# Pairs of steps added by DMA in SBUF, denominators summed once in four steps, and seven score buffers, in a two-layer graph kernel

## What is computed

```python
h = relu(layernorm(x))                                 # x: 4096 x 64
scores = (h @ W @ a1)[:, None] + (ent @ W @ a2)[None, :]
e = where(scores > 0, scores, 0.2 * scores)            # leaky relu
e = where(adj > 0, e, -9e15)
x = x + elu(softmax(e, axis=1) @ ent + h)              # first layer: attention
h = relu(layernorm(x))
x = x + (adj == 1) @ h + h                             # second layer: sum over neighbours
```

## Time and profile before

| | |
|---|---|
| three runs | 381.06, 383.52, 385.39 us (median 383.52) |
| the profiled execution | 383.43 us, of which the span from first to last instruction is 381.6 us |
| TensorE busy | 348.8 us, 91% of the span |
| VectorE busy | 271.9 us, 71% |
| ScalarE busy | 206.8 us, 54% |
| GpSimd busy | 75.7 us, 20% |
| mean granted TensorE clock | 0.982 of full speed |

### The profile page before, as it was taken

One profiled execution on the slowest core, in us unless ns is written; L12 is line 12 of the kernel. 1 busy time (PEld: TensorE's weight loads), 2 busy tenths in 40 slices (PEclk: granted clock), 3 DMA queues, 4 the chain that ended last, 5 costly groups with the idle time before them and its releaser, 6 DMA issues.

```text
span 381.6 us, 5734 instructions
## 1 busy us (share of the span) xinstructions
PE 348.8 (91%) x2377; PEld 127.6 (33%) x2377; DVE 271.9 (71%) x334; ACT 206.8 (54%) x266; POOL 75.7 (20%) x118
## 2 busy tenths in 40 slices
PE   1598897899878999998998999999999999999996
PEld 1355331123311232332322433332333333335564
DVE  2834949998689898779789776797987977522211
ACT  1120745977567779735767857257668656512100
POOL 5471583222122012022020300000008200001200
PEclk9968899999999999999999999999999999999999
DMA  6999999999999995056029000000000000000011
GB/s 181 182 106 108 108 108 107 107 108 109 106 107 108 106 107 54 2 55 57 0 15 96 3 0 2 0 2 1 2 0 2 0 2 0 2 0 2 2 55 57
DMA packets 10409, 20.67 MB, mean 54 GB/s; under 512 B 1232, under 2 KB 1296, under 8 KB 10128
## 3 DMA queue, kind: packets, MB, share of 16 engines
q0 software_dynamic: 9216, 16.78, 44.3%
q1 hardware_dynamic: 1168, 3.52, 2.5%
HBM read 69.58 MB, written 1.05 MB: 185 GB/s over the span
## 4 chain that ended last, share of the span: by engine, by line
PE 51%; DVE 11%; ACT 4%; issue 3%
PE pb L1223 17%; PE pb L1135 10%; PE pb L1244 9%; PE pa L1135 8%; DVE yp L916 5%; ACT yp L684 2%; DVE coded L828 2%; PE pa L1035 1%; PE pa L1109 1%; PE pa L1103 1%; DVE gmax L797 1%; DVE um L804 1%; PE pa L1099 1%; PE pa L1012 1%; ACT vx L576 1%
## 5 line engine op out<-in xcount | busy, mean ns | idle before, releaser
L684 ACT ACTIVATE yp<-yp,tbias,delta 128x1024 f32<-128x1024 f32 (+1 forms) x160 | 163.6, 1066 | 78.0 <-DVE yp L916 77.9
L916 DVE SCALAR_TENSOR_TENSOR yp<-s8b,t8neg,coded 128x1024 f32<-128x1024 f32 (+1 forms) x160 | 165.7, 1081 | 24.4 <-PE pb L1244 23.2
L1223 PE MATMUL pb<-yp,enta 128*64 128x512 f32 x512 | 136.4, 616 | 15.3 <-ACT yp L684 15.2
L1244 PE MATMUL pb<-yp,onesf 128*32 128x512 f32 x512 | 68.2, 605 | 0.0
L1135 PE MATMUL pb<-am,h 128*64 128x512 fp8e4 x480 | 61.7, 379 | 0.0
L451 POOL DMA_DIRECT2D am<-adj_t x64 | 34.7, 551 | 110.5 <-DMA am<-adj_t 63.2
L1223 PEld LDWEIGHTS pb<-yp,enta 128*64 128x64 f32 x512 | 28.6, 136 | 80.4 <-ACT yp L684 49.0
L1135 PEld LDWEIGHTS pb<-am,h 128*64 128x64 bf16 x480 | 29.1, 110 | 45.1 <-issue 33.5
L828 DVE TENSOR_TENSOR coded<-am,vx 128x2048 uint16<-128x2048 uint16 x32 | 38.9, 1217 | 1.1 <-ACT vx L576 1.1
L513 POOL TENSOR_SCALAR rstd<-rstd 128x8 f32<-128x8 f32 x4 | 3.7, 931 | 157.6 <-ACT rstd L617 157.6
L1135 PE MATMUL pa<-am,h 128*64 128x512 fp8e4 x288 | 34.8, 380 | 0.0
(11 more groups left out here) (165 smaller groups left out, 222.1 us busy)
## 6 DMA issues: line engine op xcount, KB each, us to landing
am<-adj_t POOLq DMA_DIRECT2D x64, 256.0 KB, 26.6
enta<-ent SPq DMA_DIRECT2D x1, 1040.0 KB, 5.1
xs<-xt SPq DMA_DIRECT2D x1, 1024.0 KB, 11.6
out<-yp SPq DMA_DIRECT2D x4, 256.0 KB, 2.0
mats<-eye SPq DMA_DIRECT2D x1, 320.0 KB, 7.1
num<-w_t SPq DMA_DIRECT2D x1, 32.0 KB, 2.0
a_sb<-a_cols SPq DMA_DIRECT2D x1, 0.5 KB, 2.0
```

The source lines that it names most:

```text
L684: e = sc.activation(y, y, ACT.Exp, bias=tbias[:, at:at + 1], scale=delta[:, 0:1])
L916: y = v.scalar_tensor_tensor(out=yp[:, n % YS, r * HALF:r * HALF + W], in0=s8b[:, pair(b) % 2, cols(b)], scalar=t8neg[:, at:at + 1], in1=c ...
L1223: t.matmul(acc2(b)[s * D:(s + 1) * D, :], enta[:, at, 0:D], yp[:, n % YS, s * HALF:(s + 1) * HALF], start=(jt == 0), stop=final, tile_posi ...
L1244: mm = t.matmul(dens[at:at + 32, :], onesf[:, 0:32], yp[:, (n - 1 + r) % YS, s * HALF:(s + 1) * HALF], start=(jt == 1), stop=final, tile_p ...
```

## The change

From step 48 on (`ADD_FROM`), in every group of four steps (4g to 4g+3) that isn't the last of its block, GpSimd issues two DMAs (`add_up`): each adds the buffer of an even step to that of the odd step behind it, in SBUF, after TensorE has done the product of the odd step (`y_read`). Seventeen groups are treated so (12 to 14, 16 to 22, 24 to 30). TensorE sums the denominators of such a group from the two sums in one round, which stands in step 4g+6 (`LAG` = 3), and then counts `pv_done` up by 4. The last group of each block (15, 23, 31) is summed in its own step 4g+3, from all four buffers, in two rounds. VectorE waits for the DMA where it writes over an even step's buffer, and for `pv_done` where it writes over an odd one's. There are 7 score buffers; for their room there are 27 slots instead of 28, and `coded` has one half, so that `put_codes` waits for the scores before it.

```diff
-SLOTS = 28
-YS = 5
+SLOTS = 27
+YS = 7
+ADD_FROM = 48
+LAG = 3
...
+    def closes(g):
+        return 4 * g + 4 in start_of
+
+    ADDED = [g for g in range(STEPS_ALL // 4) if 4 * g >= ADD_FROM and not closes(g)]
+
+
+    def sum_of(n):
+        return 2 * ADDED.index(n // 4) + n % 4 // 2
+
+    def added_by(k):
+        return k % 2, 16 * (k // 2 + 1)
...
-        coded = sb("coded", [P, 2, UNIT], U8)
+        coded = sb("coded", [P, UNIT], U8)
...
+            def add_up(n):
+                k = sum_of(n)
+                pool.wait_ge(y_read, k + 1)
+                if k >= 2:
+                    pool.wait_ge(added[k % 2], 16 * (k // 2))
+                pool.dma_start(yp[:, n % YS], yp[:, (n - 1) % YS], accum_op=ALU.add).then_inc(added[k % 2], 16)
+
             q = 24
             for n in range(STEPS_ALL):
                 b, jt = block_at(n)
+                if n // 4 in ADDED and n % 2 == 1:
+                    add_up(n)
                 while q < NC and load_step(q) <= n:
...
+                if U:
+                    dve.wait_ge(y_made, steps_of(U))
...
-                if n >= YS:
+                if n >= YS and (n - YS) // 4 in ADDED and (n - YS) % 2 == 0:
+                    k, full = added_by(sum_of(n - YS))
+                    dve.wait_ge(added[k], full)
+                elif n >= YS:
                     dve.wait_ge(pv_done, n - YS + 1)
...
+            def denominators(b, of, opens, final, done):
...
+                for i, n in enumerate(of):
+                    r = i % 2
+                    for s in range(2):
+                        at = r * D + s * 32
+                        mm = t.matmul(dens[at:at + 32, :], onesf[:, 0:32], yp[:, n % YS, s * HALF:(s + 1) * HALF],
+                                      start=(opens and i < 2), stop=(final and i >= len(of) - 2),
+                                      tile_position=(0, at))
+                mm.then_inc(pv_done, done)
...
+                if n // 4 in ADDED and n % 2 == 1:
+                    mm.then_inc(y_read, 1)
...
-                if jt % 2 == 1:
...
+                if n // 4 not in ADDED and (n % 4 == 3 if n >= ADD_FROM else n % 2 == 1):
+                    since = n - 3 if n >= ADD_FROM else n - 1
+                    denominators(b, range(since, n + 1), since == start_of[b], final, n + 1 - since)
+                if n % 4 == LAG - 1 and n // 4 - 1 in ADDED:
+                    g = n // 4 - 1
+                    for i in (1, 3):
+                        k, full = added_by(sum_of(4 * g + i))
+                        pe.wait_ge(added[k], full)
+                    denominators(b, (4 * g + 1, 4 * g + 3), 4 * g == start_of[b], False, 4)
```

More of the change, by code:

```diff
@@ L371, in graph_layers @@
         pv_done = sem("pv_done")
+        y_read = sem("y_read")
+        added = [sem(f"added{k}") for k in range(2)]
         den_sb = sem("den_sb")
@@ L827, in put_codes @@
                 t = 2 * tiles(b)
-                v.tensor_tensor(coded[:, U % 2].bitcast(U16).rearrange("p (t i) -> p t i", t=t),
+                if U:
+                    dve.wait_ge(y_made, steps_of(U))
+                v.tensor_tensor(coded[:].bitcast(U16).rearrange("p (t i) -> p t i", t=t),
                                 am[:, slot_of[U]].bitcast(U16).rearrange("p (t i) -> p t i", t=t),
@@ L916, in _ @@
                     y = v.scalar_tensor_tensor(out=yp[:, n % YS, r * HALF:r * HALF + W], in0=s8b[:, pair(b) % 2, cols(b)],
-                                               scalar=t8neg[:, at:at + 1], in1=coded[:, unit_at(b, c // 2) % 2, e:e + W].bitcast(I8),
+                                               scalar=t8neg[:, at:at + 1], in1=coded[:, e:e + W].bitcast(I8),
                                                op0=ALU.max, op1=ALU.add)
@@ L1076, in lone_rows @@
                              tile_position=(0, i * 32))
+            def denominators(b, of, opens, final, done):
+                if opens:
+                    if b >= 1:
+                        pe.wait_ge(den_sb, 2 * b)
+                    else:
+                        pe.wait_ge(h0_ready, 2)
+                for i, n in enumerate(of):
[6 more added lines that the diff above has]
+                mm.then_inc(pv_done, done)
             def combined():
@@ L1222, in _ @@
                     at = 2 * jt + s if single(b) else jt
-                    t.matmul(acc2(b)[s * D:(s + 1) * D, :], enta[:, at, 0:D],
-                             yp[:, n % YS, s * HALF:(s + 1) * HALF],
-                             start=(jt == 0), stop=final, tile_position=(0, s * D))
+                    mm = t.matmul(acc2(b)[s * D:(s + 1) * D, :], enta[:, at, 0:D],
+                                  yp[:, n % YS, s * HALF:(s + 1) * HALF],
+                                  start=(jt == 0), stop=final, tile_position=(0, s * D))
+                if n // 4 in ADDED and n % 2 == 1:
+                    mm.then_inc(y_read, 1)
                 for p, f in NORM.items():
```

## The result

The changed kernel takes 395.5 us (median; 394.9 to 396.2) against 383.8 for the one before, a ratio of 1.033 (95% interval 1.028 to 1.037). The profiled execution's span is 394.2 us against 381.6, 12.6 us more. The forecast was 386 us, in a range of 376 to 402.

A forecast was written before the change was run, and what follows sets the result against it. TensorE was taken to bound the kernel (busy 91% of the span). Rounds removed, gates, lost cover and shadow summed by blocks to +2.4 us, DMAs 0, on the 383.5 us median: 386 us, range 376 to 402.

The forecast's parts named there:

- late sums: Rival: sums land later than 6.3 us after issue, TensorE waits before 17 rounds; 390 to 408 us, chance 0.27.
- the two signs of being wrong: TensorE waits in front of L1122 for a DMA, or the chain stays on TensorE alone.
- Rounds and gate: From step 48: seventeen rounds fewer, -19.4 us; VectorE's score of step 4g+8 waits for step 4g+6's round, 1.31 us each.
- the clean group: Four steps with the wait for the buffer: 8.49 us, against 8.32 before and 7.18 without that wait.
- Less cover: At steps 77 and 109, ScalarE's finishing work no longer hidden by buffers: about 1.05 and 1.45 us.
- Rounds in the shadow of another chain: Behind steps 63, 95 and `biggest` (54, 86), removing rounds lengthens a wait: +2.9 in steps 64 to 79, +2.75 in 96 to 111.
- The room: Seven buffers before step 48: 0, between -1 and +0.5 us.
- the single half of the codes: One half of `coded`: some 0.1 us where the codes are on the chain, within the rounding.
- The DMAs: A group's second sum has 6.3 us from issue to landing; taken as 5.0, in time, at no cost.
- The landing of a lone sum: A sum by DMA lands 5.0 us after issue, as a lone 1 MB load does; bounds 2.0 and 7.0 us.
- Neither shows: Loads ahead in GpSimd's queue, four before step 69's sum, two before step 75's (about 2 us late), cost nothing.
- The slow rival's price by round: Each us beyond 6.3 waited for before 17 rounds: landing at 7.0 costs 13 us (399 us), at 7.5 20 (406).

The follow-up runs named there:

- Experiments 3: Changed kernel with 8 score buffers, 26 slots and twelve late loads cut to 64 of 2048 columns: 376.8 us, ratio 0.985 to the kernel before.
- experiment 1: Changed kernel with the last ten loads (steps 53 to 74) cut to 64 of 2048 columns: 387.7 us, ratio 1.016 to the kernel before.
- experiment 4: Changed kernel with 6 score buffers, 28 slots and the eight late loads cut to 64 columns, a single execution: 448.8 us.
- experiment 7: Complete changed kernel, late loads moved, groups 16 to 19 without sums by DMA: 8 buffers 377.5 us, ratio 0.987; 7 buffers 385.0 us, ratio 1.007.
- Experiment 5: Kernel before with only 7 score buffers, 27 slots and one half of the codes, no sums by DMA: 383.7 us, ratio 1.0036.
- experiment 2: Changed kernel with each sum by DMA cut to 16 of 1024 columns, all loads whole: 388.3 us, ratio 1.016 to the kernel before.

## Why the forecast was in range, and what in it was wrong

The measured 395.5 us is 9.5 above the forecast of 386. It lies in 376 to 402 only because the upper part of the range was kept for late sums, and these were late for another reason than that rival gave. So it was in part luck that the range held. One of the two signs of being wrong came true: TensorE waits in front of L1122 for a DMA.

*Rounds and gate* were right. Seventeen rounds went (376 instructions), the gate took them back, and the clean group is 8.49 us to the hundredth. Experiments 3, 1 and 4 show the gate as the cause: 8, 7 and 6 buffers, each traded for a slot of the adjacency, give 374, 385 and 447 us of span with small late loads (some 20 of the last 62 are the lower clock); experiment 7 shows it again with all loads whole.

*Less cover* was right in place and size. For ScalarE's exponentials the product of step 109 waits 1.06 us and that of step 110 another 0.33, where 1.45 was forecast. That of step 77 waits 0.44 in the changed kernel, at the lower clock, and 1.06 in experiment 1, where the clock is full; 1.05 was forecast.

*Rounds in the shadow of another chain*: steps 80 to 127 gave +3.8 us against +3.15 forecast. No experiment took these rounds alone, so the split between shadow and gate is only argued.

*The room* was put at 0, between -1 and +0.5, and the single half of the codes within the rounding. Experiment 5 has 1.1 to 1.4 us for both together.

*The DMAs* hold the step that failed. The landing of a lone sum was right (4.5 to 4.6 against 5.0, and within 0.2 of the 4.4 that the Trainium skill's figures gave, DMA: Bandwidth & Descriptors, Anatomy of one DMA). Wrong was "Neither shows", on the loads ahead of the sums in the queue: I had priced the four loads ahead of step 69's sum at ten us and called its round five steps off, and stopped there. The next sum queues behind that one, the sum of 71 lands at 222.2, and its round was ready at about 219. I had also left out that the sums hold up the loads, and the two loads at steps 53 and 57. In place of nothing it cost 6.4 us by the ratios and 9.2 by the profiled spans (experiment 1), of 12.6 in all. I had looked at TensorE only; VectorE, which waits for sums by the change itself, stood 6.28 us for that of step 69. Of the rivals, "the sums land late" came true in part: not in front of 17 rounds but of three (steps 58, 62 and 74, 7.5 us together), and not because adding is slow. The issue of a sum takes 0.86 us and not 0.55; no wait comes from it.

*The slow rival's price by round* was linear. Behind the waits of 3.61 and 3.14 us the clock fell (0.66 of it granted in 224 to 230 us), which put 0.9 us more on the path at step 74. I had no such term.

## What to carry to other kernels

Count buffers in steps between giving back and next use, not in buffers: batching the release of four by one semaphore behind the last of them made seven buffers tighter than five had been, and 8 instead of 7 turned +0.7% into -1.3%. A DMA with a deadline of a few us must not share a queue with bulk loads that can be issued ahead of it; place the loads where no sum is needed soon, or leave the work on the engine while loads run. And compare medians before spans: one profiled execution at a better clock made experiment 1 look 3 us better than its ratio.

## What the runs showed of the hardware that I had not expected

- An adding DMA in SBUF, 512 KB of float32 onto 512 KB, lands 4.5 us after its issue, with 0.85 us of issue on GpSimd (a load: 0.55); one of 8 KB lands after 2.0.
- Late loads in the changed kernel also took 0.87 us to issue, instead of 0.55. They were issued right behind a sum, 0.54 us after its start. In the complete kernel with eight buffers of experiment 7, the four loads at 195.7 us, with no sum right ahead, took 0.55 to 0.57, and in experiment 2, right behind tiny sums, the loads took 0.87 to 0.90 as well (the last two, 0.94 us after a sum's start, 0.55). So it goes with the place behind a sum and not with the sum's size; why is open.
- Stalls of TensorE of 2.68 us (experiment 4) were followed by a lower granted clock in seven cases of thirteen, once at 0.50 for about 6 us. In the clean groups of the changed kernel, with stalls of 1.1 us, it stayed at 1.00 (315 to 350 us).
- VectorE's score took 2.37 us instead of 1.28, and `xs` 2.00 instead of 0.69, while GpSimd did an addition of 1.42 us (experiment 7).
